# Attention layer of a four-layer kernel: scores in 64-row tiles, denominators by DMA, counts by TensorE

## The reference, cut to what matters

```python
Q, K, V = (proj(Wq, bq), proj(Wk, bk), proj(Wv, bv))
lam = LAMBDA_MAX * jnp.exp(-ALPHA * u_prev.reshape(Bb))
use_sparse = lam >= SPARSE_THRESHOLD
scores = jnp.einsum('bhqd,bhkd->bhqk', Q, K) * scale
bias = lam[:, None, None, None] * prior_bias[None, None]
dense_out = jnp.einsum('bhqk,bhkd->bhqd', jax.nn.softmax(scores + bias, axis=-1), V)
idx = prior_indices[:Ss]
s_scores = jnp.einsum('bhsd,bhskd->bhsk', Q, K[:, :, idx]) * scale
...
sparse_out = jnp.einsum('bhsk,bhskd->bhsd', jax.nn.softmax(s_scores, axis=-1), V[:, :, idx])
out = jnp.where(use_sparse[:, None, None, None], sparse_out, dense_out)
return out.transpose(0, 2, 1, 3).reshape(Bb, Ss, Dd) @ Wo.T + bo
```

## Time and profile before

| | us |
|---|---|
| median of 3 runs (lowest, highest) | 2219.41 (2218.94, 2220.04) |
| span of the profiled execution | 2220.5 |
| TensorE busy, products | 2051.3 (92%) |
| VectorE busy | 1699.0 (77%) |
| ScalarE busy | 1196.2 (54%) |
| GpSimd busy | 796.4 (36%) |
| attention layer | 0 to about 938 |

### The profile page before, as it was taken

One profiled execution on the slowest core, in us unless ns is written; L12 is line 12 of the kernel. 1 busy time (PEld: TensorE's weight loads), 2 busy tenths in 40 slices (PEclk: granted clock), 3 DMA queues, 4 the chain that ended last, 5 costly groups with the idle time before them and its releaser, 6 DMA issues. The chain is left out here.

```text
span 2220.5 us, 42789 instructions
## 1 busy us (share of the span) xinstructions
PE 2051.3 (92%) x14158; PEld 1652.1 (74%) x14158; DVE 1699.0 (77%) x2530; ACT 1196.2 (54%) x2428; POOL 796.4 (36%) x589
## 2 busy tenths in 40 slices
PE   3899999999999999759999999999995999999998
...
GB/s 92 106 106 107 107 110 110 108 109 108 105 105 106 108 109 104 24 25 1 0 0 0 0 0 0 0 0 0 0 0 59 78 79 70 85 69 80 85 66 60
DMA packets 121171, 137.47 MB, mean 62 GB/s; under 512 B 24240, under 2 KB 89776, under 8 KB 121136
## 3 DMA queue, kind: packets, MB, share of 16 engines
...
## 5 line engine op out<-in xcount | busy, mean ns | idle before, releaser
L366 DVE TENSOR_REDUCE a_neg_max<-a_s 128x2 f32<-128x512 f32 x512 | 329.1, 683 | 123.4 <-PE a_s L613 121.8
L487 ACT ACTIVATE a_e<-a_t 128x512 f32<-128x512 f32 x512 | 281.2, 610 | 228.4 <-PE a_t L626 228.4
L375 DVE SCALAR_TENSOR_TENSOR a_e<-a_e,a_w_t 128x1024 f32<-128x1024 f32 x256 | 373.6, 1469 | 4.1 <-ACT a_e L487 4.1
L613 PE MATMUL a_s<-a_k_st,a_q_st 96*128 96x256 f32 x1024 | 275.4, 380 | 0.0
L613 PEld LDWEIGHTS a_s<-a_k_st,a_q_st 96*128 96x128 f32 x1024 | 203.5, 199 | 13.7
L610 PE MATMUL a_s<-a_add_m,ident_bf 128*128 128x512 bf16 x512 | 201.8, 394 | 7.9 <-POOL a_add_m L254 5.8
L1695 ACT ACTIVATE c_hid<-c_pH,c_b 128x256 f32<-128x256 f32 x256 | 107.4, 471 | 186.3 <-PE c_pH L1758 185.9
L897 POOL TENSOR_TENSOR b_decayed<-b_table,b_mod_t 128x1024 f32<-128x1024 f32 x64 | 118.6, 1872 | 210.3 <-ACT b_mod_t L1163 203.0
L1317 PE MATMUL b_pS<-b_gated_t,b_decayed 128*128 128x256 f32 x768 | 189.5, 390 | 0.7
L626 PE MATMUL a_t<-a_q_st,a_k_st 97*128 97x512 f32 x512 | 177.1, 426 | 2.6 <-DMA a_q_st<-a_max_row 2.0
L642 PE MATMUL a_v<-a_e,a_v_pad 128*32 128x256 f32 x2048 | 163.6, 392 | 4.5 <-DVE a_e L375 2.1
...
## 6 DMA issues: line engine op xcount, KB each, us to landing
a_q_st<-a_q_hi SPq DMA_DIRECT2D x256, 128.0 KB, 2.4
a_k_st<-a_k_hi SPq DMA_DIRECT2D x256, 64.0 KB, 2.0
a_q_st<-a_q_lo SPq DMA_DIRECT2D x128, 128.0 KB, 2.4
...
a_k_st<-a_k_lo SPq DMA_DIRECT2D x128, 64.0 KB, 2.1
...
```

What stands on the lines that cost most here:

```text
L366: dve.tensor_reduce(neg_max[:, qc, head:head + 2], ps_s[b][:], AX.X, ALU.max, negate=True).then_inc(red_done, 1)
L375: dve.scalar_tensor_tensor(out=buf[:], in0=buf[:], scalar=BIG, in1=w_t[par][:, kc].unsqueeze(1).to_broadcast([P, 4, S]), op0=ALU.min, op1= ...
L487: act.activation(e[g % E_BUFS][:, 2 * b:2 * b + 2], ps_t[b][:], ACT.Exp).then_inc(exp_done, 1)
L613: ins = pe.matmul(ps_s[b][:, r], q_st[par][0:96, slot, qc * P:qc * P + P], k_st[par][0:96, slot // 2], start=False, stop=(r == 1))
```

## The change

`trace_layer` and `expert_and_final` stay as they are. In `attention_layer`:

1. **Scores in two row tiles.** The heads are dealt in another order (`heads`, `slots`: wv, bv and wo on the host), so that two heads lie 64 partitions apart. q and k share one tensor `st`; a term takes 16 rows, three terms 48 rows, and the maxima stand in the 49th. The even and odd copies of q and `par_mask` go. `score_rows` and `score_cols` issue four products of 256 columns in turn to rows 0 to 48 and rows 64 to 112 of the array, each half with its PSUM bank. All terms of both halves are now 12 DMAs a `stack`, of 16 rows and 1024 elements a row; eight of them wait for the low parts. The maxima take two DMAs.
2. **Order on TensorE.** `score_cols(n, g)` stands ahead of `project_q` and `project_k`. `transpose_max` no longer waits for the spread reciprocals.
3. **Denominators by DMA.** `collect`, `spread`, `combine` and the copies `even` and r_rep go from PE, DVE and ACT. GpSimd sends the rows of sums to memory (`den_rows`, two DMAs), reads them back as 128 x 32 (`den`), VectorE takes the reciprocal of that, GpSimd sends it to memory (`r_rows`) and reads it back repeated over each head's 16 channels (`r_rep`). ScalarE issues four DMAs (`merge`) that put the odd heads' values of `raw_v[1]` into `raw_v[0]`. `normalize` moves from g = 4 to g = 5.
4. **Counts by TensorE.** The block that loads the constants goes, and two constants are loaded with the rest. VectorE writes 64 one-hot tiles (`hot`, bfloat16, 256 columns), and 64 products with the identity add them up in `ps_v[0]`.
5. **Merged copies.** `high_parts` and `low_parts` each take q and k in one operation of 1024 elements a row; `whole_q` is two operations instead of four, `values` two instead of four. `low_parts` waits for the landing of both stacks of the batch before.

The core of the diff:

```diff
         def stack(n, par, half):
             sp.wait_ge(stack_free[half], n + 1)
...
+            for done, term, first, step in ((hi_done, 0, 1, 1), (lo_done, 1, 1, 2), (lo_done, 2, 0, 2)):
                 sp.wait_ge(done, n + 1)
-                for term in terms:
+                for r in range(2):
                     for j in (2 * half, 2 * half + 1):
...
+                        rows = split[64 * r + 16 * j:64 * r + 16 * j + 16, first:first + step + 1:step].bitcast(F32)
+                        sp.dma_start(st[par][64 * r + 16 * term:64 * r + 16 * term + 16, :, j].bitcast(F32), rows)\
+                          .then_inc(d_stack[half], 16)
...
         def maxima(n, par):
             sp.wait_ge(mrow_done, n + 1)
-            sp.dma_start(q_st[par][96:97].bitcast(F32), max_row[:].bitcast(F32)).then_inc(d_max, 16)
+            for r in range(2):
+                sp.dma_start(st[par][64 * r + 48:64 * r + 49, 0].bitcast(F32), max_row[8 * r:8 * r + 8].bitcast(F32))\
+                  .then_inc(d_max, 16)
...
         def low_parts(n):
-            pool.wait_ge(khi_done, n + 1)
-            pool.tensor_tensor(k_lo[:], k_full[:], k_hi[:].bitcast(F32), ALU.subtract).then_inc(klo_done, 1)
-            pool.wait_ge(qhi_done, n + 1)
-            pool.tensor_tensor(q_lo[:], q_full[:], q_hi[:].bitcast(F32), ALU.subtract).then_inc(qlo_done, 1)
+            pool.wait_ge(hi_done, n + 1)
+            if not (isinstance(n, int) and n == 0):
+                for half in d_stack:
+                    pool.wait_ge(half, n * 16 * STACK_DMAS)
+            pool.tensor_tensor(split[:, 0::3], full[:], split[:, 1:3].bitcast(F32), ALU.subtract).then_inc(lo_done, 1)
...
+        def denominators(n):
+            at_least(pool, d_den, n * 16)
+            for half in range(2):
+                pool.wait_ge(raw_done, 2 * n + half + 1)
+                pool.sem_inc(pool_seen, 1)
+                pool.dma_start(den_rows[:, half], raw_v[half][16 * (1 - half)::32].rearrange("j c s -> j (c s)")).then_inc(d_row, 16)
+            pool.wait_ge(d_row, 32 * (n + 1))
+            at_least(pool, rden_done, n)
+            pool.sem_inc(pool_seen, 1)
+            pool.dma_start(den[:], den_rows.rearrange("j h (m k) -> (j h m) k", k=32)).then_inc(d_den, 16)
+        def spread(n):
+            pool.wait_ge(rden_done, n + 1)
+            at_least(pool, d_rep, n * 16)
+            pool.sem_inc(pool_seen, 1)
+            pool.dma_start(r_rows.rearrange("j h (m k) -> (j h m) k", k=32), rden[:]).then_inc(d_r, 16)
+            pool.wait_ge(d_r, 16 * (n + 1))
+            at_least(pool, att_done, n)
+            pool.sem_inc(pool_seen, 1)
+            pool.dma_start(r_rep[:].rearrange("p c s -> p (c s)"),
+                           r_rows.rearrange("j h s -> (j h) s").unsqueeze(1).to_broadcast([8, DH, C * S])).then_inc(d_rep, 16)
...
         def body(n, par, proj, maxi, finish):
+            if finish:
+                denominators(n - 1)
             if proj:
                 masks(n + 2, par)
+            if finish:
+                spread(n - 1)
             if maxi:
                 weights(n + 1, 1 - par)
...
+        def reciprocal(n):
+            dve.wait_ge(d_den, 16 * (n + 1))
+            at_least(dve, d_r, 16 * n)
+            dve.reciprocal(rden[:], den[:]).then_inc(rden_done, 1)
...
+        def merge(n):
+            act.wait_ge(d_row, 32 * (n + 1))
+            act.wait_ge(raw_done, 2 * (n + 1))
+            for j in range(4):
+                act.dma_start(raw_v[0][32 * j + 16:32 * j + 32], raw_v[1][32 * j + 16:32 * j + 32]).then_inc(d_merge, 16)
...
-                    ins = pe.matmul(ps_s[b][:, r], q_st[par][0:96, slot, qc * P:qc * P + P],
-                                    k_st[par][0:96, slot // 2], start=False, stop=(r == 1))
+                    rows = slice(64 * r, 64 * r + 48)
+                    ins = pe.matmul(ps_s[r][:, c], st[par][rows, 0, j, c, qc * P:qc * P + P], st[par][rows, 1, j, c],
+                                    start=False, stop=(c == C - 1), tile_position=(64 * r, 0))
...
+            for c in range(C):
+                for r in range(2):
+                    rows = slice(64 * r, 64 * r + 49)
+                    ins = pe.matmul(ps_t[r][:, c], st[par][rows, 1, j, c, kc * P:kc * P + P], st[par][rows, 0, j, c],
+                                    start=True, stop=True, tile_position=(64 * r, 0))
...
+        def count(k):
+            for j in range(K_SPARSE):
+                pe.wait_ge(hot_done, k * K_SPARSE + j + 1)
+                pe.matmul(ps_v[0][:, k], ident_bf[:], hot[:, j], start=(j == 0), stop=(j == K_SPARSE - 1)).then_inc(hot_mm, 1)
```

414 lines of the change are left out of this document (166 added, 248 removed).

## The result

The changed kernel takes 2341.9 us (median of 4 runs, 2341.05 to 2343.24) where the kernel before takes 2219.72 on the same chip: 1.0549 times as long, 95% interval 1.0534 to 1.0564. It is slower, as forecast, but by 122 us and not by 64, and 7 us outside the range. The profiled execution's span is 2339.6 us, against 2220.5.

The account below looks back on a forecast made before the run. TensorE's work was taken to bound the kernel before, a DMA ring the changed one: 28 laps x (29.3 - 27.03) = +63.6 us, setup -6, tail +8, ends -2, giving 2283 us; range 2200 to 2335 us.

Parts of the forecast that it names:

- The ring: Maxima, reciprocal, GpSimd's denominator DMAs, weights, low_parts, stack DMAs, next maxima: one lap a batch, 27.7 us at full clock.
- Leg 1: From the landed maxima to the reciprocal's end, on TensorE and VectorE: 8.8 us of the lap.
- SyncE with the landing: Ten DMA issues up to the last of the maxima, 6.3 us, and its landing 2.2: 8.6 us with hand-overs.
- GpSimd's: Lap term: r_rows out and landed 2.5 us, r_rep issue 0.8, weights 4.56, low_parts 2.37; 10.3 us with hand-overs.
- The clock: TensorE's waits at the batch boundary lower its clock on project_q and row scores: 1.6 us more, lap 29.3 us.
- The start: Setup: first scores near 42 us, 2.2 us a group, first maxima near 60 us: -6 us (bounds -10, +1).
- The tail: Layer's end: four DMA hops of 2.5 us replace 4.3 us of products: +8 us.
- What TensorE saves: Per batch: 3.8 us from overlapping row tiles in the scores, less 1.2 us for layout changes.
- The slack: In the kernel before, TensorE's work sets the batch's pace; queues, GpSimd and SyncE have slack.
- Faster: Rival: small DMAs close the lap under VectorE's floor, clock stays up, 25.3 us a batch, 2171 us; chance 0.18.
- a floor of 25.3 us: VectorE's work, about 22.8 us with stretched weighings, plus TensorE's last values and first row scores between batches.
- Slower still: Rival: row tiles run one after the other, or GpSimd's hops take 3.3 us: lap 30.7 to 31, 2326 us; chance 0.11.

Follow-up runs that it names:

- e1: Changed kernel with low_parts(n+2) moved ahead of weights(n+1) on GpSimd, right behind the DMA of r_rep; 2255.0 us.
- e4: Changed kernel with the denominators left out and r_rep set to 1 once, so the output is not normalized; 2197.0 us (one run).
- e5: Changed kernel with project_q(n+2) at the very start of a batch, ahead of the first row scores, and its x loaded between high and low stack DMAs; 2304.3 us.
- e7: Changed kernel with the denominators carried by TensorE again as before; row tiles, order, merge and setup stay; 2240.9 us.
- e9: Changed kernel with denominators on TensorE again and project_q(n+2) ahead of the column scores of g = 0; 2234.9 us.
- e6: Kernel before with two more subtractions of 512 elements on GpSimd ahead of each k_lo of the loop; 2255.2 us.
- e11: Changed kernel with low_parts ahead of weights, project_q between row and column scores of g = 0, x loaded between high and low stack DMAs; 2246.0 us.
- e13: Kernel before with only the denominators changed to DMAs, in the changed kernel's GpSimd order; 96-row scores stay; 2307.1 us.

## Why the prediction was right in its mechanism and wrong in its size

- **The ring** was right: it closes in the trace, leg by leg, and e1, e4, e5 and e7 each cut it at another place and got 38 to 145 us back. The signs named for it came too: 30.5 us between the maxima (over 29), a clock under 1.00, TensorE's waits for the maxima and the stack, and 222.7 us in which SyncE waits for low_parts in 100 to 900 us. TensorE's busy share is 85%, not some 80.
- **Its size** is the step that failed: 1.6 us a lap too small at the full clock, 29.3 against 27.7. Leg 1 was 9.2 against 8.8, SyncE with the landing 8.6 as forecast. The term that was mis-sized is GpSimd's, 11.6 us against 10.3: low_parts lasts 2.80 and not 2.37 us, weights with r_rep's issue 5.7 and not 5.4, and the queue takes 0.6 us to go on after the reciprocal, where 0.1 was put for all hand-overs. 1.6 x 28 = 45 us, by far the most of the 55 us that the span was off.
- **The clock** was right in kind and nearly in size: 30.8 - 29.35 = 1.4 us a lap on average, forecast 1.6. It falls on 14 of 25 laps, which are 2.5 us longer on average, 2.1 of it in the first leg; one of the 14 also lost 3.0 us in GpSimd's queue.
- **The start** was wrong by 7 us. The first row scores begin at 43.5 us, as forecast (42), 9 earlier than before. But a group then takes 2.7 us and not 2.2: TensorE waits 0.8 us in each, and its granted clock is 0.50 from 43 to 65 us (the last row is this window):

```profile
46.02 1.20 PE L599 MATMUL a_s<-a_add_m,ident_bf 128*128 128x512 bf16 x2 [0.79 <-DVE a_top L383]
47.16 0.79 PE L603 MATMUL a_s<-a_st 48*128 48x256 f32 x4
...
47.99 1.29 DVE L383 TENSOR_REDUCE a_top<-a_s 128x2 f32<-128x512 f32 x2 [1.42 <-PE a_s L603]
...
48.73 1.21 PE L599 MATMUL a_s<-a_add_m,ident_bf 128*128 128x512 bf16 x2 [0.79 <-DVE a_top L383]
...
43.00:65.00 22.00, 15.17 (x48) 5.59 (x48) 9.76 (x16) 1.06 (x1) 13.21 (x14) 0.50 0.41 64
```

- **The tail** came as forecast, +8.5 for +8, in part by luck: the terms given, four hops of 2.5 us for 4.3 us of products, make 5.7. From the last values' copy to the residual's end it is 1055.1 - 1035.8 = 19.3 us, against 12.2 in the earlier trace rows, so 7.1 of the 8.5 us are there:

```profile
1035.80 0.60 ACT L491 ACTIVATE a_raw<-a_v 128x512 f32<-128x512 f32 x1 [0.96 <-PE a_v L634]
...
1053.88 1.25 POOL L271 TENSOR_TENSOR x_all<-a_delta,x_all 128x512 f32<-128x512 f32 x1 [8.72 <-ACT a_delta L461]
```

- **What TensorE saves** was too large in the forecast: 1.6 us in the scores less 1.2 around them is 0.4, where 2.6 was put, because each change of tiles costs more than the 0.07 to 0.11 us of the forecast. It didn't matter for the changed kernel, whose batch the ring sets, but it is why e9, which keeps the tiles and drops the DMAs, is not faster than the kernel before.
- **The slack** that the first paragraph gives to GpSimd in the kernel before was wrong: in e6 2.5 us more of GpSimd cost 1.1 us a batch, through a weighing. That TensorE's own work sets the pace there was right (26.7 of 27.0 us).
- **"Faster"** rested on a floor of 25.3 us. The terms listed for it add up to 22.8 + 0.57 + 0.78 = 24.2, and the runs show it too low even so: with no denominators at all (e4) most batches take 25.8 us. In e11 the lap is some 23 us by the sum of its legs (8.2 to the reciprocal, 6.8 on GpSimd, 8.1 as in e5 for SyncE and the landing), far under the floor, and most batches take 26.5 us and others up to 32.3.
- **"Slower still"**, at 2326 us, is the rival nearest to the measured time, by neither of its mechanisms: the tiles overlap, and r_rep is issued 2.4 to 3.3 us after r_rows, where a longer landing was made up by a shorter stretch behind it (8.2 us from the issue of r_rows to low_parts in nearly every lap).

What stays open: what sets the batch of the kernels that keep the DMAs with the ring cut. VectorE's idle time is 5.1 to 6.4 us a batch in e1, e4, e11 and e13, and 3.6 before; TensorE is busy only 87 to 91% there, and a part is its lower level (a clock of 0.94 to 0.98). For e7 and e9 (5.9 and 5.2 us, at a clock of 1.00) TensorE's own work is most of the answer, at 95 and 97% busy. That both masks of a group now wait for both reductions was not tested by itself, nor were the four merges. None of the kernels that were run beats the kernel before and still computes the denominators.
